# Seven unread matrix products ahead of and between the first transposes of a fused conv and attention block

## The chip, the cores and the metric

The kernel runs on one core of a Trainium2 chip. The metric is the device time of one execution in microseconds; the time of a kernel is the median of its runs. TensorE (PE in the profile) does the products and transposes, VectorE (DVE), ScalarE (ACT) and GpSimd (POOL) the elementwise work, SyncE (SP) issues most of the loads and stores.

## The reference

For x (32 x 32 x 256, batch x time x channel) and cond (32 x 256), with biases and weights in float32, the reference computes:

```python
x = x + causal_depthwise_conv(x, cond)            # 32 lags; cond holds one weight for each lag and channel
ada = cond @ ada_w + ada_b                        # shift1, scale1, gate1, shift2, scale2, gate2
x1 = layernorm(x) * (1 + scale1) + shift1
q, k, v = split(x1 @ qkv_w + qkv_b)               # 16 heads of 128
o = softmax(q @ k.T / sqrt(128)) @ v              # within each batch of 32 tokens
x_a = x + gate1 * (o @ out_w + out_b)
x2 = layernorm(x_a) * (1 + scale2) + shift2
out = x + (x_a + gate2 * (gelu(x2 @ ffn_w1 + ffn_b1) @ ffn_w2 + ffn_b2))
```

## The kernel before

Every engine has its own program, written out by hand, and the programs meet at semaphores. The 1024 tokens are worked on with channels on the partitions (two channel tiles, ct 0 and 1). They are split in two halves of 512, and the first half in two chunks of 256.

**How it starts.** GpSimd writes the constants: `ident` (a 128x128 identity, L289 to L292, raises `s_const` to 1), `ones` (128x128, every element 1/256, L293, raises it to 2) and `mhalf` (L294, raises it to 3). ScalarE issues the load of `crow` (cond, L363), SyncE those of x in three chunks (`xtok`, L219), of the first part of `ada_w` (L222), of the biases (`rows`, L245) and of the first weights. TensorE waits for `ident` and `crow` and transposes cond (L896). VectorE copies the result to `condT` (L553). TensorE then transposes x's first two chunks, four transposes each, as they land (L903), into the banks `OB` and `YB`; VectorE (L564) and ScalarE (L389) copy channel tile 0 and 1 of each to `x0`.

**The convolution of the first half.** The 32 lags are shared out. VectorE does fourteen of them in both channel tiles as multiply-and-add steps into `xc` (L559, L584), in a chain. TensorE does eighteen as products with a diagonal matrix (L917, function `conv` of the TensorE program), in the order of lags 14, 31, 15, 30 and so on to 22, 23, into two banks: a lag j takes 16 x (32 - j) columns, in each of the two channel tiles, so that two lags that follow each other make up 304 columns for each channel tile whatever the pair. The diagonals `diag` are made from `ident` and `condT` by ScalarE (L379, 27 of them) and GpSimd (L300, nine). An f32 product stands in the trace as two matmul instructions, a transpose as one. Between its lags TensorE transposes the second half of x (L1093, when its load has landed), makes the first modulation rows (L969, from `adaw`), turns the biases (L1100) and the modulation rows (L977).

**Behind it.** VectorE adds TensorE's bank to `xc` (L598, function `conv_sum`), which needs its own chain of steps and TensorE's last lag. `conv_sum` releases the layer norm of the first chunk: mean by a product with `ones` (L936), the modulation's additions (L666, L673), centring (L614), squares on ScalarE (L405), variance (L945), reciprocal root on GpSimd (L316), spreading (L961), scaling and shifting (L640, L647), rounding (L415), and then the projections (L1028 and on). In the gaps of that chain TensorE does three lags of the second half (L917 again). GpSimd's first splitting of weights (L306) waits for the first `conv_sum` too. The rest is eight rounds of projections, attention and output projection, and two feed-forward layers. `PB[1]` is one of three banks for projections; its first use in the kernel before is the projection of tile 1.

Of the kernel before, what the change touches and what calls it, by code (L numbers as in the profile page):

```python
# [11 lines left out]
P = 128  # L12
# [4 lines left out]
def cond_resid_block_kernel(nc, x, cond, ada_w, ada_b, qkv_w, qkv_b, out_w, out_b,  # L17
# [53 lines left out]
    with ExitStack() as ctx:  # L71
        def sb(name, shape, dt=F32):
            return ctx.enter_context(nc.sbuf_tensor(name, shape, dt))

        def sem(name):
            return ctx.enter_context(nc.semaphore(name))
# [21 lines left out]
        ident = sb("ident", [P, P])  # L98
        ones = sb("ones", [P, P])
# [32 lines left out]
        PB, S_BANK, OB, YB = banks[0:3], banks[3], banks[4:6], banks[6:8]  # L132
# [5 lines left out]
        s_const, s_id0, s_zero = sem("constants_set"), sem("ident_zeroed"), sem("pt_zeroed")  # L138
# [751 lines left out]

        @block.tensor
        def _(pe):
            pe.wait_ge(s_const, 1)
            pe.wait_ge(s_row[0], 16)
            for ct in range(CT):
                m = pe.transpose(S_BANK[:, B * ct:B * (ct + 1)], crow[:, ct * P:(ct + 1) * P], ident[0:B, 0:B])  # L896
# [1 line left out]
            for n in range(2):  # L898
                t0, nt = CHUNKS[n][0] // P, CHUNKS[n][1] // P
                pe.wait_ge(s_x[n], 16)  # L900
                for ct in range(CT):
                    for t in range(nt):
                        m = pe.transpose((OB, YB)[n][ct][:, t * P:(t + 1) * P], xtok[:, t0 + t, ct * P:(ct + 1) * P], ident[:, :])  # L903
                m.then_inc(s_xt, 1)

            def conv(n, i0, i1):
                last = len(PE_LAGS[n]) - 1
                for i in range(i0, i1):
                    j = PE_LAGS[n][i]
                    d = DIAG_LAGS.index(j)  # L910
                    for ct in range(CT):
                        if (d, ct) in BY_POOL:
                            pe.wait_ge(s_diag[1], BY_POOL.index((d, ct)) + 1)
                        else:
                            pe.wait_ge(s_diag[0], BY_ACT.index((d, ct)) + 1)
                        xs = by_batch(half(x0, ct, n))
                        m = pe.matmul(by_batch(CONV_BANK[n][ct][:, :])[:, :, j:], diag[:, CT * d + ct, :],  # L917
                                      xs[:, :, :T - j], start=(i == 0), stop=(i == last))
                        if i == last:
                            m.then_inc(s_cpe, 1)  # L920
# [367 lines left out]
```

## Time and profile before

| what | us |
|---|---|
| median of three runs | 313.19 |
| the three runs | 311.98, 313.54, 313.19 |
| profiled execution, its own time | 314.73 |
| its span, first to last instruction | 312.9 |
| TensorE busy | 302.3 |
| VectorE busy | 177.7 |
| ScalarE busy | 174.4 |
| GpSimd busy | 119.5 |

The span is what the trace covers; the 1.8 us between it and the profiled execution's own time lie outside the instructions. Busy time of TensorE is that of its matmuls, whose ends are modelled: they overlap, so a start-to-start distance says more than a duration.

### The profile page before, as it was taken

The numbers are of one execution on the slowest core, as the hardware profiler recorded it, in microseconds if no ns is written. First come the engines' busy times: TensorE is split into PE (matmuls) and PEld (weight loads), VectorE is DVE, ScalarE is ACT, GpSimd is POOL, SyncE is SP. The second block draws the span as 40 slices with busy tenths as digits, with TensorE's granted clock in tenths as the row PEclk, the third lists the DMA queues.
The fourth block names the chain that finished last, engine by engine and source line by source line (L and its number), as shares of the span: only waits on it lengthen the run. The fifth ranks groups of instructions, "written<-read, shape, count | busy, mean of one in ns | idle before, by whom it ended". The sixth has DMA issues, their size and how long they took to land.

```text
span 312.9 us, 6154 instructions
## 1 busy us (share of the span) xinstructions
PE 302.3 (97%) x2604; PEld 255.2 (82%) x2604; DVE 177.7 (57%) x304; ACT 174.4 (56%) x316; POOL 119.5 (38%) x103
## 2 busy tenths in 40 slices
PE   4998999999999999999999999999999989999995
PEld 3896897887888888888888888888898868878885
DVE  3985798888768555453446553340620555757232
ACT  5454567543762856376367636644762793725901
POOL 5105646630823364064327224630911492311400
PEclk9999999999999999999999999999999999999999
DMA  6902240600080052007003400520180000000012
GB/s 216 374 24 65 71 136 2 196 7 0 3 270 0 2 164 107 1 4 266 3 2 112 159 2 2 180 90 0 33 304 2 2 0 3 0 0 1 2 67 67
DMA packets 15275, 23.00 MB, mean 74 GB/s; under 512 B 808, under 2 KB 8336, under 8 KB 15248
## 3 DMA queue, kind: packets, MB, share of 16 engines
q1 hardware_dynamic: 15200, 22.58, 21.4%
q8 instruction: 20, 0.33, 0.4%
q14 instruction: 7, 0.06, 0.1%
q10 hardware_dynamic: 48, 0.03, 0.0%
HBM read 21.57 MB, written 1.05 MB: 72 GB/s over the span
## 4 chain that ended last, share of the span: by engine, by line
PE 87%; DVE 5%; ACT 4%; POOL 2%; DMA 1%; issue 1%; DVEq 0%
PE bank L981 15%; PE bank L983 15%; PE bank L982 15%; PE bank L1068 8%; PE bank L917 5%; PE bank L989 4%; PE bank L991 4%; PE bank L990 4%; PE bank L1052 3%; PE bank L1191 2%; PE bank L1193 2%; PE bank L1192 2%; POOL wl L306 1%; PE bank L961 1%; ACT wh L374 1%; DVE xc L584 1%
## 5 line engine op out<-in xcount | busy, mean ns | idle before, releaser
L306 POOL TENSOR_TENSOR wl<-raw,wh 128x512 fp32r<-128x512 f32 x70 | 94.9, 1381 | 129.7 <-ACT wh L374 110.9
L425 ACT ACTIVATE pool<-bank,bT 128x512 f32<-128x512 f32 x56 | 38.5, 688 | 54.4 <-PE bank L983 54.4
L981 PE MATMUL bank<-x1h,wl 128*128 128x512 f32 (+1 forms) x174 | 65.6, 377 | 0.5 <-POOL wl L306 0.5
L982 PE MATMUL bank<-x1l,wh 128*128 128x512 f32 (+1 forms) x174 | 64.6, 371 | 0.0
L983 PE MATMUL bank<-x1h,wh 128*128 128x512 f32 (+1 forms) x174 | 64.6, 371 | 0.0
L707 DVE SCALAR_TENSOR_TENSOR ol<-bank,bT,oh 128x512 fp32r<-128x512 f32 x32 | 24.0, 750 | 37.4 <-ACT oh L450 36.3
L584 DVE SCALAR_TENSOR_TENSOR xc<-x,condT,xc 128x496 f32<-128x496 f32 (+27 forms) x82 | 43.3, 597 | 0.1
L374 ACT ACTIVATE wh<-raw 128x512 fp32r<-128x512 f32 x70 | 39.8, 622 | 0.0
L981 PEld LDWEIGHTS bank<-x1h,wl 128*128 128x128 f32 x174 | 32.8, 189 | 6.5 <-POOL wl L306 1.0
L983 PEld LDWEIGHTS bank<-x1h,wh 128*128 128x128 f32 x174 | 32.7, 188 | 5.7
L982 PEld LDWEIGHTS bank<-x1l,wh 128*128 128x128 f32 x174 | 32.8, 188 | 5.3
L1068 PEld LDWEIGHTS bank<-pt,pool 128*128 128x128 f32 x256 | 32.1, 191 | 3.7 <-issue 1.9
L1068 PE MATMUL bank<-pt,pool 128*128 128x128 f32 x256 | 32.5, 275 | 1.5 <-DVE ol L707 1.5
L450 ACT ACTIVATE oh<-bank,bT 128x512 fp32r<-128x512 f32 x32 | 22.0, 687 | 10.9 <-PE bank L1068 10.9
L981 PE MATMUL bank<-oh,wl 128*128 128x512 f32 x64 | 26.7, 418 | 0.2 <-DVE ol L707 0.2
L989 PE MATMUL bank<-wh,x1l 128*128 128x512 f32 x64 | 25.9, 405 | 0.0
L983 PE MATMUL bank<-oh,wh 128*128 128x512 f32 x64 | 25.1, 392 | 0.0
L991 PE MATMUL bank<-wh,x1h 128*128 128x512 f32 x64 | 25.0, 391 | 0.0
L982 PE MATMUL bank<-ol,wh 128*128 128x512 f32 x64 | 25.0, 390 | 0.0
L990 PE MATMUL bank<-wl,x1h 128*128 128x512 f32 x64 | 25.0, 390 | 0.0
L702 DVE STREAM_TRANSPOSE pt<-pnorm 32x512 f32<-32x512 f32 (+1 forms) x36 | 23.2, 644 | 1.2
L679 DVE TENSOR_REDUCE mx<-bank 128x16 f32<-128x512 f32 x8 | 5.5, 692 | 32.2 <-PE bank L1052 32.2
(136 smaller groups left out, 432.4 us busy)
## 6 DMA issues: line engine op xcount, KB each, us to landing
raw<-in_L_cond_qkv_w_dram SPq DMA_DIRECT2D x24, 512.0 KB, 5.6
raw<-in_L_cond_out_w_dram SPq DMA_DIRECT2D x8, 512.0 KB, 3.5
raw<-in_L_cond_ffn_w_dram SPq DMA_DIRECT2D x3, 512.0 KB, 6.2
adaw<-in_L_cond_ada_w_dram SPq DMA_DIRECT2D x1, 1024.0 KB, 10.6
out_dram<-pool SPq DMA_DIRECT2D x3, 256.0 KB, 2.2
xtok<-in_x_dram SPq DMA_DIRECT2D x2, 256.0 KB, 3.1
adaw<-in_L_cond_ada_w_dram SPq DMA_DIRECT2D x1, 512.0 KB, 5.7
xtok<-in_x_dram SPq DMA_DIRECT2D x1, 512.0 KB, 6.5
```

The lines of the kernel that those rows point to most:

```text
L306: g.tensor_tensor(wl[:, cols], raw[:, cols], wh[:, cols].bitcast(F32), ALU.subtract)\
L374: a.activation(wh[:, cols], raw[:, cols], ACT.Copy).then_inc(s_whi[i], 1)
L425: a.activation((q_sb if j < GH else k_sb)[:, j % GH, :], src, ACT.Identity, bias=bias(U, j // GH, j % GH)).then_inc(s_ev, 1)
L584: m = v.scalar_tensor_tensor(out=acc[:, :, j:], in0=xs[:, :, :T - j], scalar=w, in1=(acc if i else xs)[:, :, j:], op0=ALU.mult, op1=ALU.add)
L707: v.scalar_tensor_tensor(out=ol[:, h, :], in0=OB[h % 2][:, :], scalar=bT[:, row:row + 1], in1=oh[:, h, :].bitcast(F32), op0=ALU.add, op1=A ...
L981: pe.matmul(dst, wl[:, w_cols], a_hi, start=start, stop=False)
L982: pe.matmul(dst, wh[:, w_cols], a_lo, start=False, stop=False)
L983: return pe.matmul(dst, wh[:, w_cols], a_hi, start=False, stop=stop)
L989: pe.matmul(dst, x1l[:, kt, tk], wh[:, wc], start=(kt == 0), stop=False)
L990: pe.matmul(dst, x1h[:, kt, tk], wl[:, wc], start=False, stop=False)
L991: m = pe.matmul(dst, x1h[:, kt, tk], wh[:, wc], start=False, stop=(kt == CT - 1))
L1068: m = pe.matmul(OB[h % 2][:, t * P:(t + 1) * P], v_sb[:, t, h * P:(h + 1) * P], pt[:, h, t, :], start=True, stop=True)
```

## The change

TensorE's program waits for `ones` as well as for `ident` and then does four products of the two into `PB[1]`; after the eight transposes of x's first two chunks it does three more. Nothing reads them. No other engine's program is touched.

```diff
         @block.tensor
         def _(pe):
-            pe.wait_ge(s_const, 1)
+            def idle_products(count):
+
+                for _ in range(count):
+                    pe.matmul(PB[1][:, 0:P], ident[:, :], ones[:, :], start=True, stop=True)
+
+            pe.wait_ge(s_const, 2)
+            idle_products(4)
             pe.wait_ge(s_row[0], 16)
...
                         m = pe.transpose((OB, YB)[n][ct][:, t * P:(t + 1) * P], xtok[:, t0 + t, ct * P:(ct + 1) * P], ident[:, :])
                 m.then_inc(s_xt, 1)
+            idle_products(3)
```

## Rows read from the trace of the kernel before

**Rows 1.** The page: busy time of each engine, and the clock in 40 slices.

```profile
PE 302.3 (97%) x2604; PEld 255.2 (82%) x2604; DVE 177.7 (57%) x304; ACT 174.4 (56%) x316; POOL 119.5 (38%) x103
...
PEclk9999999999999999999999999999999999999999
```

**Rows 2.** Timeline from 0 to 34 us: start, length, engine, line, count.

```profile
0.74 0.45 ACTq L363 DMA_DIRECT2D crow<-in_cond_dram  x1
...
1.42 0.20 POOL L293 MEMSET ones<- 128x128 f32 x1
...
1.74 0.46 SPq L222 DMA_DIRECT2D adaw<-in_L_cond_ada_w_dram  x1
2.24 0.49 SPq L219 DMA_DIRECT2D xtok<-in_x_dram  x1
...
3.38 0.39 PE L896 MATMUL bank<-ident,crow 32*128 32x32 f32 x2 [3.38 <-DMA crow<-in_cond_dram]
...
3.76 1.97 PE L903 MATMUL bank<-ident,xtok 128*128 128x128 f32 x8
...
6.33 8.23 PE L917 MATMUL bank<-x,diag 128*128 128x288 f32 x24 [0.60 <-DVE x L564]
...
7.59 14.50 DVE L584 SCALAR_TENSOR_TENSOR xc<-x,condT,xc 128x496 f32<-128x496 f32 x26
...
16.83 2.14 ACT L379 ACTIVATE diag<-ident,condT 128x128 f32<-128x128 f32 x7
...
24.89 0.95 DVE L598 TENSOR_TENSOR xc<-xc,bank 128x144 f32<-128x144 f32 x4 [2.79 <-PE bank L917]
...
25.55 1.10 PE L936 MATMUL bank<-xc,ones 128*128 128x256 f32 x4 [0.52 <-DVE xc L598]
...
26.49 1.13 PE L917 MATMUL bank<-x,diag 128*128 128x288 f32 x4
```

**Rows 3.** The chain that ended last, its pieces from 6 to 31 us.

```profile
14.57 1.73 PE bank L1093 x8
16.30 3.40 PE bank L917 x16
19.70 0.57 PE bank L969 x16
20.28 2.45 PE bank L917 x16
...
22.79 1.09 PE bank L917 x8
...
26.07 0.75 DVE adaT L673
...
28.10 1.05 PE bank L945 x8
```

**Rows 4.** Weight loads by line, from 6.3 to 17.9 us, then from 18.4 to 24.9 us.

```profile
L917 PEld LDWEIGHTS bank<-x,diag 128*128 128x128 f32 x30 | 8.6, 334 | 2.7 <-DVE x L564 1.0
...
L917 PEld LDWEIGHTS bank<-x,diag 128*128 128x128 f32 x40 | 5.8, 190 | 0.2 <-issue 0.2
```

**Rows 5.** DMA issues up to 20 us: KB each, median us from issue to landing.

```profile
adaw<-in_L_cond_ada_w_dram SPq DMA_DIRECT2D x1, 512.0 KB, 5.7
xtok<-in_x_dram SPq DMA_DIRECT2D x1, 512.0 KB, 6.5
crow<-in_cond_dram ACTq DMA_DIRECT2D x1, 32.0 KB, 2.5
```

**Rows 6.** Two stretches of the last 2.5 us: busy times, PEclk, DMA share, GB/s.

```profile
310.50:311.70 1.20, 0.00 (x0) 0.00 (x0) 0.00 (x0) 0.14 (x1) 0.00 (x0) 1.00 0.17 56
311.80:312.90 1.10, 0.00 (x0) 0.00 (x0) 0.00 (x0) 0.00 (x0) 0.00 (x0) 0.50 0.27 80
```

**Rows 7.** TensorE's timeline: its longest idle time behind 4 us, and its last work.

```profile
258.40 1.13 PE L1068 MATMUL bank<-pt,pool 128*128 128x128 f32 x8 [1.54 <-DVE ol L707]
...
309.62 0.71 PE L1209 MATMUL bank<-ident,x 128*128 128x128 f32 x4 [0.58 <-DVE x L869]
```

## The prediction

> **What bounds the kernel now.** I read the page first: TensorE is busy for 302.3 of 312.9 us, so what it does early it does for the whole kernel: any time won at the first join is kept if the work behind it moves up as a whole [rows 1]. The seven products lie in the first 7 us, so I read the timeline of the first 34 us, then the chain that ended last there.
>
> The join of the first half's convolution is L598. VectorE's steps run without a gap from 7.59 to 22.09 us (7.59 + 14.50); L598 starts at 24.89, after 2.79 us of idle time that ends with TensorE's L917 [rows 2]. TensorE is on the chain from 6.33 until then, without a hole: 24 matmuls of the convolution in 8.23 us, eight transposes, 16 matmuls in 3.40 us, 16 in 2.45, eight in 1.09 [rows 2, 3]. Each eight of these L917 matmuls are two lags of 304 columns together, the same work: 8.23/3 = 2.74 us for eight at the start, 1.70 in the middle, 1.22 and 1.09 later. Work that is the same costs over twice as much early on. The weight loads say why: 334 ns each up to 17.9 us, 190 ns each from 18.4 us on [rows 4]. That is TensorE at 1.2 GHz and at 2.4 GHz. The clock column reads full speed everywhere [rows 1], so it shows nothing of this start, and I take the level from durations alone: low to about 18.2 us, high from there. What the engine did before the rise: convolution products without a pause from 6.33, then eight transposes at 215 ns each (1.73/8), then another 2 us of products [rows 2, 3].
>
> So the first 25 us are bounded by TensorE at half clock, and VectorE stands 2.79 us behind it. That is the most the change can bring there.
>
> **The change part by part.** *The four products* are eight matmuls of 128 columns. At the low clock the nearest row is the transposes of the same width, 215 ns each: 1.7 us [rows 3]. `ones` is written at 1.62, so they run from about 1.7 to 3.5 (the first weight load is exposed, some 0.15). cond lands at 0.74 + 2.5 = 3.24 and L896 starts at 3.38 [rows 2, 5]: it becomes 0.1 to 0.15 late, and with it `condT` and the first diagonals. The x transposes start at 3.76 behind their own load and have 0.1 us of room after L896's two small matmuls, so they are not late, nor are the copies behind them. The cover is the wait for cond; without it the four would cost 1.8 us. The raised wait (`s_const` 2 for 1) ends at 1.62, well ahead of 3.24, and costs nothing.
>
> *The three products* are six matmuls, 1.3 us at 215 ns. They start when the transposes have streamed (about 5.5) and end at 6.8; the convolution, which starts at 6.33 behind the copies [rows 2], is 0.48 us late at the low clock. At the high clock they fit in the hole: 6 x 0.11 = 0.7 us. VectorE's steps need the copies, not these products, so their chain still ends at 22.1. Nobody waits for `PB[1]` this early, and no DMA or queue of SP or POOL is passed.
>
> *The clock.* TensorE is now at work almost without a break from 1.7 us instead of 3.4, and the hole of 0.6 us ahead of the convolution is filled [rows 2]. If this brings the clock up at 5 to 9 us, TensorE's share shrinks as follows. Priced high, from 6.8: 24 matmuls, 4.1 (wide ones 0.24 apart, from 1.13 for four less the last one's tail, narrow ones 0.11 as L945's, [rows 2, 3]); eight transposes 0.9; 16 matmuls 2.5; modulation 0.57; 16 at 2.45; eight at 1.09, with the turns of biases and rows 0.2; the last eight 1.05 [rows 3]. Sum 12.8, end at 19.6; with up to 2 us of the first ones still at the low clock, 19.6 to 20.6. Nothing else holds it: x's second half lands at 2.24 + 6.5 = 8.7 and adaw at 1.74 + 5.7 = 7.4 [rows 2, 5], and the last seven diagonals, 2.14 us behind ScalarE's copies, come by about 16 [rows 2], as they are needed. So VectorE becomes the gate, at 22.15 instead of 24.89: **2.74 us won**. There is 1.5 us of room in that: the clock may come up as late as about 11 us. GpSimd's first splitting and the layer norm hang on L598 and move with it.
>
> *What the won time makes.* TensorE now idles from about 20.3 until L936, which follows L598 by 0.66 us: 22.8. That is a hole of about 2.5 us, where the longest in the trace at the high clock is 1.54 [rows 7]. At the end of the kernel the clock read 1.00 until 311.7 and 0.50 from 311.8, 1.4 us after the last product had streamed, with a hole of 0.58 us shortly before [rows 6, 7]. So the low clock can come back in the new hole. Its price: L936's four matmuls (0.85 us at the high clock) take 0.85 more, 0.15 of it hidden beside L673 [rows 3], and the four of L917 take 0.95 more, of which 0.5 lies in an idle wait for the squares: 0.95 to 1.2 us if the clock comes back within those two, I take 0.95. If it stays low through L945 (+0.85), the next L917 (+0.7) and the spreading (+0.45), 3.2; with the next lag and mean, up to 4.5; I take 3.6.
>
> A page of the Trainium skill, "TensorE: Matmul & The Clock Gate" (section "Part 1: The HAM clock gate"), says that the point of the rise differs between executions of one kernel. One trace cannot show that, but the runs allow it: 311.98 to 313.54.
>
> **Against the median.** The profiled execution took 314.73 (312.9 of span, 1.8 around it), the median is 313.19. The sum for it is 314.73 - 2.74 = 311.99. If its 1.54 us above the median are the cost of being profiled, the sum for unprofiled runs is 310.45. If they are a later rise of the clock, VectorE's 22.1 is a floor that some runs of before already touch (311.98 is just that sum), and it is 311.99. The coincidence makes me weigh the second twice: 310.45 + 2/3 x 1.54 = **311.5**.
>
> **The rivals.** *(a) Forecast*: clock up early and kept, 311.5. For it: the filled start; against it: the hole of 2.5 us. *(b) The clock drops in the new hole, briefly*: 311.5 + 0.95 = 312.4. For it [rows 6, 7]; it decides if the low level returns before 22.8. *(c) It drops and stays low to the spreading*, the case on the other side: 311.5 + 3.6 = 315.1, slower than before. Against it: L936 and L917 follow each other closely, which is much work at the low clock; it decides from 2.1 us of extra on (half against the median). *(d) The products don't bring the clock up*: the convolution starts 0.48 late and all else stays: 313.19 + 0.45 = 313.6. For it: in before, 8 us of products from 6.33 did not raise the clock [rows 2, 4]; the rise needed more than being busy. Against it: the dense part that preceded the rise held the transposes.
>
> On this last point a page's rule speaks against the change: "TensorE: Matmul & The Clock Gate", section "Part 4: PE-mode transpose", has it that transposes do not count as work for the clock. Then the eight at 3.76 would part the two groups of products, and it would come out as (d). The trace leans the other way: the rise came behind a stretch with eight transposes in it and not in the 8 us of products before. The same page's table "Why this matters for your kernels" warns of idle gaps between bursts, which is (b) and (c).
>
> **How the numbers follow.** (a) 0.36, (b) 0.32, (c) 0.13, (d) 0.19. No change that can be told is within 0.5%, 311.62 to 314.76. Faster: (a) when the profiled excess is in part profiling, and (b) when it is all that: 0.75 x 0.36 + 0.45 x 0.32 = 0.41. Slower: most of (c) and a little of (d), 0.14. Same: 0.45. The range goes from 310.3 (the lower reading of (a)) to 314.3, through (b) and (d), and leaves most of (c) out; the forecast's own range is 310.4 to 312.0.
>
> **What would show it.** Right: weight loads of L917 near 190 ns before 10 us; TensorE's last lag of the first half near 20; L598 at 22.1 to 22.2 right behind L584, with no wait for L917; L936 at 22.8; the projections (L1028) at 30.1 for 32.88. Wrong in (b) or (c): clock 0.50 somewhere from 22 us on, L936's matmuls 0.43 us apart. Wrong in (d): L917's weight loads at 334 ns beyond 14 us, the convolution from 6.8 and L598 at 25 or later. The prediction is also wrong if VectorE is late by condT, which would show in L584's start behind 7.59.

## The result, and the profile after

| kernel | median us | runs | from | to |
|---|---|---|---|---|
| before | 312.15 | 14 | 311.98 | 313.58 |
| after | 314.52 | 14 | 312.91 | 316.13 |

The ratio is 1.0055, with a 95% interval of 1.0036 to 1.0073: the change makes the kernel slower by half a per cent, or 1.7 us. (The medians lie 2.4 us apart and the means 1.8.) The profiled execution of after took 315.05 us, of which 313.2 are span. The forecast was 311.5, the range 310.3 to 314.3. The fastest execution with the products is 0.9 us slower than the fastest without them.

The timeline of the first 34 us of the changed kernel. The products are at L896, and what was L903, L917, L936, L945, L961 and L1028 is L909, L924, L943, L952, L968 and L1035.

```profile
1.68 2.08 PE L896 MATMUL bank<-ones,ident 128*128 128x128 f32 x8 [1.68 <-POOL mhalf L294]
...
3.69 0.42 PE L902 MATMUL bank<-ident,crow 32*128 32x32 f32 x2
...
4.04 1.97 PE L909 MATMUL bank<-ident,xtok 128*128 128x128 f32 x8
...
5.79 1.31 PE L896 MATMUL bank<-ones,ident 128*128 128x128 f32 x6
...
6.94 4.19 PE L924 MATMUL bank<-x,diag 128*128 128x288 f32 x24
...
7.91 14.51 DVE L584 SCALAR_TENSOR_TENSOR xc<-x,condT,xc 128x496 f32<-128x496 f32 x26
...
18.57 1.21 PE L924 MATMUL bank<-x,diag 128*128 128x160 f32 x8
22.45 0.95 DVE L598 TENSOR_TENSOR xc<-xc,bank 128x144 f32<-128x144 f32 x4
...
23.11 1.32 PE L943 MATMUL bank<-xc,ones 128*128 128x256 f32 x4 [3.33 <-DVE xc L598]
...
24.22 2.13 PE L924 MATMUL bank<-x,diag 128*128 128x288 f32 x4
...
26.14 1.71 PE L952 MATMUL bank<-ones,x 128*128 128x1 f32 x8
...
32.68 0.38 PE L1035 MATMUL bank<-x1h,wl 128*128 128x256 f32 x1
```

(L896 is `idle_products`, L902 the transposes of cond.) Against [rows 2]: the 24 matmuls of the first six lags take 4.19 us for 8.23, TensorE is through at 19.8, and L598 starts at 22.45 right behind VectorE's steps, with no idle time before it. That is 2.44 us earlier than in the profile of before. Then TensorE idles for 3.33 us, the four of L943 and the four of L924 behind it take 1.32 and 2.13 us where they took 1.10 and 1.13, and L1035 is only 0.20 us earlier than its like was, 32.88. The gain is gone before the first projection.

The clock of that stretch, from the view of stretches of time (length, busy times of the engines, then PEclk, DMA share and GB/s):

```profile
20.00:22.00 2.00, 0.00 (x0) 0.00 (x0) 2.00 (x6) 0.91 (x2) 0.00 (x0) 1.00 0.00 0
22.00:23.80 1.80, 0.69 (x3) 0.67 (x4) 1.73 (x7) 0.00 (x0) 0.75 (x1) 1.00 0.00 0
23.90:27.00 3.10, 3.10 (x11) 2.39 (x9) 1.98 (x5) 0.75 (x2) 1.65 (x2) 0.50 0.09 18
27.00:30.60 3.60, 3.60 (x13) 3.13 (x14) 0.16 (x1) 0.00 (x0) 1.96 (x2) 0.50 0.36 130
30.80:34.00 3.20, 3.20 (x19) 2.38 (x18) 2.80 (x8) 2.12 (x6) 0.83 (x1) 1.00 0.02 5
```

The clock falls to its lower level (1.2 GHz) between 23.8 and 23.9, when TensorE has just come out of the hole, and is back at 2.4 GHz between 30.6 and 30.8.

A second loss lies far behind, where nothing was changed. This is TensorE's timeline around 136 us in the changed kernel:

```profile
133.72 1.30 PE L1059 MATMUL bank<-pool 128*32 128x32 f32 x128
...
136.19 0.39 PE L998 MATMUL bank<-wh,x1h 128*128 128x512 f32 x1
137.13 0.39 PE L996 MATMUL bank<-wh,x1l 128*128 128x512 f32 x1 [0.55 <-issue]
```

Two matmuls that are some 0.23 us apart in the rows around them stand 0.94 apart, and the 0.55 us of idle time are put down to issue, which is time in which the engine waited for nothing that the profile shows. Matched one by one, TensorE's matmuls are 0.25 us earlier than in the profile of before ahead of this place, 0.42 later right behind it and 0.27 later at the kernel's end. That makes up the span: 313.2 for 312.9.

**The executions one by one.** The view of cores gives a mean granted clock and a span for each. Those of after sort by the clock; the stretch of 6.8 us at half clock in the profile above makes the mean of that execution 0.989 (6.8 x 0.5 / 313.2 = 0.011):

| mean clock | executions | span us | time us |
|---|---|---|---|
| 1.00 | 3 | 311.0 to 311.1 | 312.91, 312.92, 314.51 |
| 0.995 | 4 | 311.7 to 312.0 | 313.46 to 313.78 |
| 0.989 | 5 | 312.7 to 313.6 | 314.53 to 315.41 |
| 0.981 to 0.984 | 2 | 313.8 to 314.3 | 315.56, 316.13 |

(The 314.51 has a span of 311.0: what it lost lies outside its instructions.) By their mean clock, eleven of fourteen executions had the clock fall in mid-kernel, and it costs 0.7 to 3.3 us of span. Even those where it doesn't are 0.9 us above before's common 312.0.

### The profile page after: what moved, and what is told of

Read it like the earlier page. It is cut to its first block, busy times and chain, and to the rows that moved or that the text cites. A ratio compares the mean times of both kernels' runs of the same rounds, so it can differ in the third digit from the quotient of the medians.

```text
span 313.2 us, 6181 instructions
## 1 busy us (share of the span) xinstructions
PE 302.0 (96%) x2618; PEld 256.3 (82%) x2618; DVE 177.7 (57%) x304; ACT 174.4 (56%) x316; POOL 119.5 (38%) x103
## 4 chain that ended last, share of the span: by engine, by line
PE 83%; DVE 9%; ACT 4%; POOL 2%; issue 1%; DVEq 0%; POOLq 0%
PE bank L988 15%; PE bank L990 15%; PE bank L989 15%; PE bank L1075 8%; DVE xc L584 6%; PE bank L996 4%; PE bank L997 4%; PE bank L998 4%; PE bank L1059 3%; PE bank L1198 2%; PE bank L1200 2%; PE bank L1199 2%; POOL wl L306 1%; PE bank L968 1%; PE bank L924 1%
## 5 line engine op out<-in xcount | busy, mean ns | idle before, releaser
L997 PE MATMUL bank<-wl,x1h 128*128 128x512 f32 x64 | 24.9, 389 | 0.0
L998 PE MATMUL bank<-wh,x1h 128*128 128x512 f32 x64 | 24.9, 389 | 0.0
```

The source lines that it names most:

```text
L997: pe.matmul(dst, x1h[:, kt, tk], wl[:, wc], start=False, stop=False)
L998: m = pe.matmul(dst, x1h[:, kt, tk], wh[:, wc], start=False, stop=(kt == CT - 1))
```

## The experiments

All times are medians; each kernel with five rounds has 10 to 12 executions, beside 28 to 35 of the kernel before on the same chip.

**The kernel before once more (e1_before_again, e12_before_third).** No edit.

> The kernel before, unchanged, for the clock of each of its executions. Theory A (the profiled execution of before was one of its slow cases; in most executions TensorE's clock rises early enough that VectorE is the gate at 22.1): most executions near 312.1 us with a span near 310.3, some near 313.5, few near 314.7; the profile, if it catches a common one, has L598 at 22.2. Theory B (profiling costs the 2.6 us between 314.73 and 312.15, and L598 stands at 24.9 in every execution): every profile again has L598 at 24.9 and a span near 312.9.

> A third profile of the kernel before, one look. Theory A (its executions differ by when TensorE's clock rises): whichever class it falls in, the time and L598 go together: L598 at 22.2 with 311.9, or TensorE's last lag and L598 near 23.5 with 313.3 (the class that has no profile yet), or L598 at 24.9 with 314.7. A time of 313.3 with L598 at 22.2 would mean that this class has another cause.

Measured: 311.98 (ratio 0.9998, 0.9978 to 1.0017), its profiled execution 312.01; and 313.10 for the single execution of e12. The rows of the two timelines, first that of 312.01, then that of 313.10:

```profile
6.32 6.02 PE L917 MATMUL bank<-x,diag 128*128 128x288 f32 x24 [0.60 <-DVE x L564]
...
7.58 14.50 DVE L584 SCALAR_TENSOR_TENSOR xc<-x,condT,xc 128x496 f32<-128x496 f32 x26
...
22.11 0.95 DVE L598 TENSOR_TENSOR xc<-xc,bank 128x144 f32<-128x144 f32 x4
22.78 1.10 PE L936 MATMUL bank<-xc,ones 128*128 128x256 f32 x4 [1.80 <-DVE xc L598]
```

```profile
6.34 8.23 PE L917 MATMUL bank<-x,diag 128*128 128x288 f32 x24 [0.61 <-DVE x L564]
...
14.37 1.42 PE L1093 MATMUL bank<-ident,xtok 128*128 128x128 f32 x8
...
23.40 0.95 DVE L598 TENSOR_TENSOR xc<-xc,bank 128x144 f32<-128x144 f32 x4 [1.29 <-PE bank L917]
```

Theory A holds. With the profile of [rows 2] there are three: L598 at 22.11, 23.40 and 24.89, times of 312.0, 313.1 and 314.7. The steps agree to 0.2 us (1.29 and 1.49 at L598, 1.1 and 1.6 in the time). The 24 first matmuls tell when the clock rose: during them (6.02 us), behind them (8.23, with L1093 at 1.42 us), or later still (8.23, L1093 at 1.93 us). Of the 96 executions of before that ran beside the experiments, 57 lie at 311.7 to 312.4, 37 at 313.0 to 313.8 and two at 314.6. Each group has one profile, and the others are put into it by their time alone. By that, the profile that the prediction was made from shows one of the rarest. In the common one VectorE is the gate already, TensorE idles for 1.80 us, and there is nothing for the change to win.

**Four, or three (e2_only_four, e3_only_three).** One line less in each.

```diff
-            idle_products(3)
```

is the edit of e2 to the changed kernel, and that of e3

```diff
-            idle_products(4)
```

> Keeps the four products ahead of cond, drops the three after the transposes. If the loss is made of a clock that rises early and falls in the hole ahead of L943 (hole theory), the rise is less sure and later, the hole shorter, and the time lies between before and after: 312.4 to 314. If it is made of cond and x being 0.3 us late alone (late theory), the four carry all of it: every execution at or above 312.4, and the same as with all seven.

> Keeps the three products after the transposes, drops the four. cond and x are not late: the 0.3 us are gone. Hole theory: executions still fall in classes by the clock, 312.1 without a drop, 0.8 to 3 us more with one. Late theory: 312.1 in all of them. The wait of 0.7 us at issue near 136 us that the profile of the changed kernel has: if it comes from the number of TensorE's instructions it can go or move here.

Measured: four alone 312.14 (ratio 1.0018, 0.9995 to 1.0041), three alone 311.89 (1.0000, 0.9981 to 1.0020). With the four no execution is below 312.06, where before has 311.74: 0.3 us, in all of them. With the three the fastest is 311.76. Neither has the wait at issue near 136 us. Three of twelve executions of e2 have a fall of the clock in mid-kernel (mean clock 0.992 and 0.982, 313.1 to 315.1) and four of e3 (0.993 to 0.987, 312.8 to 314.3). e3's profile fell on one of these: its stretch from 23.60 to 30.20 reads 0.50, as in the changed kernel. So the late theory accounts for 0.3 us and no more, and each group of products alone brings some falls. In the profile of e2 the hole is 1.56 us and the clock stays; in that of e3 it is 3.32.

**The hole filled (e4_fill_hole).**

```diff
             conv(0, 16, len(PE_LAGS[0]))
+            idle_products(11)
             mean(0)
```

> The changed kernel with eleven more unread products between TensorE's last lag of the first half and the mean (22 matmuls, 2.4 us at the high clock), so that there is little of the hole of 3.3 us left. Hole theory: the clock column stays at 1.00 after its rise, and the executions of 313.5 to 316 vanish: all near 312.9. If the drop has another cause, the classes stay as they are, with a median of 314.5. Where the clock is late the eleven are paid in full, 2.4 us.

Measured: 312.14 (0.9996, 0.9982 to 1.0009), and every one of twelve executions between 312.05 and 312.22. It has all seven products of the change and eleven more, and none of its executions falls in mid-kernel. TensorE's rows around the hole:

```profile
19.40 2.62 PE L896 MATMUL bank<-ones,ident 128*128 128x128 f32 x22
23.10 1.10 PE L943 MATMUL bank<-xc,ones 128*128 128x256 f32 x4 [1.08 <-DVE xc L598]
```

The hole is 1.08 us for 3.33, and no clock falls: the hole is what lets it fall. The time was 0.8 less than expected, because a second thing differs from the change: its wait at issue near 136 us is not in this kernel. That wait can't be what brings the fall, which comes at 23.9 us in the changed kernel, long ahead of it.

**Needed work in the hole (e5_work_in_hole).**

```diff
-            mean(0)
             pe.wait_ge(s_xe[2], CT)
-            conv(1, 0, 1)
+            conv(1, 0, 2)
+            mean(0)
             var(0)
-            conv(1, 1, 2)
             spread(0)
```

> The changed kernel with all seven products, and with two lags of the second half's convolution, work that is needed anyway, moved from behind the mean and the variance into the hole ahead of the mean (2 us at the high clock). Hole theory: with the hole down to about 1.3 us the clock is kept in most executions, and those of 313.5 and more are gone; the moved work leaves smaller holes later, which may cost a drop in a few. If only the unread products' own count matters, nothing changes against the 314.5 of the change. TensorE has as many instructions as in the changed kernel: if the 0.7 us of issue near 136 us come from the count, they are here too, and the time is 312.8; without them 312.1.

Measured: 313.81 (1.0033, 1.0015 to 1.0052), a miss. All twelve executions have a fall (mean clock 0.995 to 0.989), and the wait at issue is in the profile too (two matmuls 0.78 us apart at 134.45). The rows:

```profile
23.11 1.10 PE L943 MATMUL bank<-xc,ones 128*128 128x256 f32 x4 [1.39 <-DVE xc L598]
25.66 1.05 PE L952 MATMUL bank<-ones,x 128*128 128x1 f32 x8 [1.44 <-ACT x L405]
27.76 1.22 PE L968 MATMUL bank<-ident,rs 128*128 128x128 f32 x4 [1.06 <-POOL rs L316]
```

One hole of 3.33 us became three of 1.39, 1.44 and 1.06, with matmuls of one column in L952 between two of them, and the clock fell ahead of L968, whose four matmuls take 1.22 us for 0.71. The length of the longest hole alone doesn't decide: before keeps its clock over 1.80 us in e1, and the kernel of e8 over 2.34.

**Three, and the hole filled (e6_three_fill, e11_three_fill_11).** As e4, without the four, with nine and with eleven products in the hole.

> The three products after the transposes, nine in the hole, none ahead of cond. Hole theory with the late theory for the 0.3 us of the four: every execution at the floor of VectorE's chain, 311.7 to 312.1, so a narrower spread than before and a mean 0.4 lower, with a median about the same as before's 312.0. If the four are needed for an early rise, some executions come out at 313 and more.

> Three products after the transposes and eleven in the hole, none ahead of cond: 28 more instructions than before, where 24 more showed a wait of 1.6 us at the scores of the third round. Fetch theory: the wait differs from that of 24 more by the place alone, between nothing (311.8) and 2 us (313.8), and is the same in every execution of this kernel. If the wait came from the hole's products, it is 1.6 us again.

Measured: with nine 314.22 (1.0064, 1.0040 to 1.0089), a miss; with eleven 312.07 (0.9983, 0.9969 to 0.9998). In the profile of the first, L1058, the scores of a later round:

```profile
131.21 1.26 PE L1058 MATMUL bank<-pool 128*32 128x32 f32 x124
134.34 0.26 PE L1058 MATMUL bank<-pool 128*32 128x32 f32 x4 [1.87 <-issue]
```

A stall of 1.87 us for four instructions, with nothing to wait for. It is absent with eleven. The seven of its ten executions without a fall lie at 313.7 to 314.3, 1.6 to 2.3 us above 312.07, so the stall seems to be in each of them. The other three lie at 315.6 to 315.9 with a mean clock of 0.992 to 0.995: they have a fall although nine products stand in the hole (0.61 us is left of it in the profile). No profile shows where that fall is; the stall is one candidate. Eleven executions of e11 are at 312.00 to 312.18 and one at 312.22; the mean is 312.08, that of before on the same chip 312.70. It is the only kernel that beats before beyond its interval, and it does it by having one class instead of two.

**Transposes instead of products (e7_transposes).**

```diff
-                    pe.matmul(PB[1][:, 0:P], ident[:, :], ones[:, :], start=True, stop=True)
+                    pe.transpose(PB[1][:, 0:P], ones[:, :], ident[:, :])
-            idle_products(4)
+            idle_products(8)
-            idle_products(3)
+            idle_products(6)
```

> The changed kernel with eight and six unread transposes of the constants instead of the four and three products, one matmul instruction each, of the same 128 columns. If the clock counts transposes like products, it rises at 5 to 9 us and the classes of the change return (clock 1.00, 0.995, 0.989, median near 314.5). If transposes do not count, as the page on TensorE has it, the rise comes where it came without the seven products or later: 312.1 to 314 with no drop, clock 1.00.

Measured: 313.79 (1.0038, 1.0014 to 1.0063), with the classes of the change: mean clock 1.00 (312.36 to 312.61), 0.995 and 0.992 (313.5 to 313.9), 0.989 (314.4 to 315.0), 0.981 (315.5). Its first 24 matmuls take 4.19 us, to the digit as long as those of the change:

```profile
6.92 4.19 PE L924 MATMUL bank<-x,diag 128*128 128x288 f32 x24
```

So unread transposes do what unread products do: nothing but transposes ran ahead of these 24. The kernel has as many instructions as the change, and its profile has the wait too, at the same matmul. It is small, 0.50 us from start to start for 0.23, and so no idle time is put down to it:

```profile
135.90 0.39 PE L998 MATMUL bank<-wh,x1h 128*128 128x512 f32 x1
136.40 0.39 PE L996 MATMUL bank<-wh,x1l 128*128 128x512 f32 x1
```

**One product more (e8_plus_one).** `idle_products(4)` for the three.

> The changed kernel with four instead of three products after the transposes: two more matmul instructions and two more weight loads. Hole theory: the same classes by the clock as in the change. If the 0.7 us at issue near 136 us hang on where TensorE's instructions lie in what is fetched, they can be gone, and each class lies 0.65 lower: 312.3 without a drop, 313.0 with one, near 314 with two. If they belong to the early rise or to the lost time, they stay.

Measured: 314.12 (1.0058, 1.0031 to 1.0086); classes as in the change, spans of 311.1 to 311.4 at clock 1.00. The wait at issue is still there (0.6 us idle, at L997). It did not go away with two more instructions, and it stands two matmuls nearer to the 128 small ones, which two more at the start have pushed back. The profile is one at clock 1.00. Its clock rose later than in the changed kernel's (24 matmuls in 4.62 us for 4.19), and its hole is shorter:

```profile
7.50 4.62 PE L924 MATMUL bank<-x,diag 128*128 128x288 f32 x24
...
23.10 1.10 PE L943 MATMUL bank<-xc,ones 128*128 128x256 f32 x4 [2.34 <-DVE xc L598]
```

It fits that the same kernel loses its clock in one execution and keeps it in the next: falls stand in the profiles with holes of 3.25 to 3.33 us, none in those with 2.34 and less in one piece.

**The seven in the hole, none at the start (e9_seven_in_hole).** The kernel before with the function `idle_products`, and ahead of `mean(0)`:

```diff
+            pe.wait_ge(s_const, 2)
+            idle_products(7)
             mean(0)
```

> The kernel before with the same seven unread products, all of them between TensorE's last lag of the first half and the mean, and none ahead of the convolution: the clock then rises as in the kernel before, cond is on time, and no hole grows. Fetch theory (the 0.7 us of issue near 134 us come from 14 more instructions ahead of that place, which move where a block of TensorE's program begins): the wait is there, and each class of before lies 0.5 to 0.8 higher, 312.5 and 313.9. If the wait comes with the early rise, it is absent and the common class stays at 311.9. In the late class, where there is no hole for them, the seven cost 1.5 us more.

Measured: 313.23 (1.0028, 1.0008 to 1.0048). No fall of the clock in mid-kernel; the five fastest executions lie between 312.40 and 312.78, the first of them 0.4 above before's 312.01, and the slowest four at 313.97 to 314.78, above all of before's late ones, 313.2 to 313.75; three lie between. The profile is a late one (24 matmuls in 8.23 us); there the seven cost 0.8 us, the mean at 24.83 for the 24.06 of e12, where 1.5 were expected. The wait at issue is in the profile again (0.4 us idle at L994). It comes with instructions put ahead of it, whatever the clock does.

**Two, three and thirteen (e10_two_three_fill).** Two products ahead of cond for the four, the three after the transposes, and thirteen ahead of `mean(0)`.

> Two products ahead of cond, three after the transposes, thirteen in the hole: as many instructions as in the kernel with eleven in the hole (36 more than before), which had no wait at issue, but cond not late. Fetch theory: no wait near 134 us, as there. Late theory: 0.3 us less than 312.14 in every execution, 311.85, with no drop of the clock and a spread under 0.3 us. If thirteen are too many for the hole, L943 starts late and the time stays at 312.1 or more.

Measured: 312.45 (0.9997, 0.9984 to 1.0010), 311.98 to 312.85. No wait at issue and no fall. cond is on time, and L598 starts at 22.14, but thirteen are too many: they run 3.06 us from 20.41, and L943 starts at 23.31 where before has 22.78. What the two saved the thirteen gave back.

## Why the prediction was wrong

**What bounds the kernel.** Right for the execution it was read from, wrong for the kernel. "TensorE at half clock is the bound, VectorE stands 2.79 us behind it" holds in two of 96 executions, as their times sort them; in 57 VectorE is the gate, and in 37 TensorE is by 1.3 us (e1, e12). The prediction saw this reading (314.73 - 2.74 is within 0.01 of the fastest run, 311.98) and gave it two thirds. It is all of it: profiling cost nothing, e1's profiled 312.01 stands beside a median of 311.98. By that reading the forecast would have been 312.0, no change, at best. The median that it was set against, 313.19 of three executions, is 312.15 with fourteen.

**The clock comes up early.** Right. TensorE's first 24 matmuls took 4.19 us; the prediction had 4.1 at the high clock and said that up to 2 us of them may be low. TensorE's last lag ended at 19.8, forecast 19.6 to 20.6. The convolution started at 6.94, forecast 6.8. Rival (d) did not come. Transposes alone, put in the products' place, gave the same 4.19 us and the same classes (e7). The Trainium skill, "TensorE: Matmul & The Clock Gate", section "Part 4: PE-mode transpose", says that they do not count for the clock; this case's trace does not agree with it for f32.

**The four are covered.** Mis-sized. Forecast was 0.1 to 0.15 us late for cond and nothing for x. The eight matmuls, priced at 1.7 us, took 2.08 from 1.68, L902 started at 3.69 for 3.38, and L909 at 4.04 for 3.76, so x was late too, and VectorE's chain with it: 7.91 for 7.59, L598 at 22.45 for 22.15. That is the 0.3 us that e2 has in every execution and e3 in none.

**2.74 us won.** Against its own profile of before it was 2.44 at L598, the 0.3 off. Against most executions it was -0.3.

**The clock is kept (case a).** This is the step that failed. The hole was forecast at 2.5 us and measured at 3.33 (TensorE through early, L598 late), and the low clock came back in 11 of 14 executions. Cases (b) and (c) were the right mechanism: together 0.45 against 0.36 for (a), yet the forecast went by (a), because (b) and (c) were counted apart. The price was estimated at 0.95 for a short fall and 3.6 for a long one; measured were 0.7 to 1.0 of span at mean clock 0.995, 1.7 to 2.6 at 0.989 and 2.8 to 3.3 at 0.98. e4 shows that the hole is the cause: filled, none of twelve executions falls, nor any of the 24 of e10 and e11.

**Not foreseen at all:** the wait at issue, 0.7 us in the profile. That it is in every execution of this kernel is not shown, but the times add up with it: 312.0 (before's common case) + 0.3 (late start) + 0.7 (issue) = 313.0, measured 312.91 and 312.92 without a fall; with the commonest fall, 1.7, it is 314.7 for a median of 314.52. Against the forecast of 311.5 that is 0.5 for the bound that most executions do not have, 0.3 and 0.7 for the two delays, and 1.7 for the clock.

**Where the wait at issue comes from.** Counted from the start of TensorE's program, the matmul behind it is the 1233rd in all six profiles that have it (change, e5, e6, e7, e8, e9), with 14, 16 or 24 matmul instructions put in ahead. So it is bound to a place in the program, and the kernel's own work slides past that place. The instruction transfers of queue 8 are 16 KB each, and they go with TensorE's program: the pages count 20 of them in the kernels with up to 16 more instructions and 21 in those with 24 and more. The row of the changed kernel from 128 to 140 us (packets, MB, share):

```profile
q8 instruction: 2, 0.03, 0.9%
```

The first of these two is the ninth of the kernel. In the six profiles the 1233rd matmul starts 1.34 to 1.54 us after the ninth transfer has landed (change: landed at 135.58, start at 137.13). In the other eight it comes 2.4 to 7.6 us after, and nothing waits. In the profiles of before the 128 small products are its matmuls 1085 to 1212, and 20 wide ones lie between them and this place, which is time enough. With 14 more it is six, with 24 more the place lies among the small products, four from their end, and the stall is longest. With 28 or more the ninth transfer lands at 124.9 to 126.2, 6 us and more ahead of the 1233rd matmul. So TensorE waits there for the next piece of its program. The traces fit this in all fourteen profiles; no run moved the transfer itself.

**Open.** What starts the ninth transfer when it does. Open too is what exactly lets the clock fall or stay: 1.08 us in e4, 1.80 in before (e1) and 2.34 in e8 did no harm, three of 1.39, 1.44 and 1.06 did (e5), and three executions of e6 fell with most of the hole filled.

## What to carry to other kernels

Before an early stall is costed from one profile, see whether the executions agree: where times lie in groups (here 312.0, 313.2, 314.6), the profile shows one group, and what can be won is what the common one has. Raising TensorE's clock early did not pay here, since work that finishes earlier in front of a fixed gate turns into idle time, and the low clock came back where it cost more. If unread products are used at all, they belong in the hole too, and they must be few enough for it. Even then they only took away the late group of executions (e11: a mean of 312.08 for 312.70) and left the common time as it was. Each build has to be timed, since instructions that cost nothing where they stand can cost 0.3 to 2 us at issue elsewhere. Where a matmul waits for nothing that the profile shows, count its number in the engine's program and look when the instruction queue's last transfer ahead of it landed.

## What was not expected of the hardware

- The same program on the same chip has three times, some 1.3 us apart (311.7 to 312.2, 313.0 to 313.5, 314.6 beside e5 to e8). By the three profiles they differ in when TensorE's clock first rises; the clock column reads 1.00 for all three, because it shows nothing ahead of the first rise. Durations show it: weight loads of 334 and 190 ns [rows 4].
- A handful of instructions in the first 25 us brings a stall of 0.3 to 2 us over 100 us later, with no engine, semaphore or load named for it. It ends 1.34 to 1.54 us after a transfer of TensorE's instruction queue has landed, at the same matmul of the program in six kernels.
- Transposes raise the clock as products do: 4.19 us for the first 24 matmuls behind either (e7).
